# Attention with a LoRA gate on one core: row sums gathered by GpSimd and DMA, eleven probability buffers, gate weights loaded late, PSUM banks split 3 and 4

## The reference

```python
xn = layernorm(x)
q, k, v = xn @ wq, xn @ wk, xn @ wv          # 32 query heads, 8 key/value heads, 32 wide
k, v = repeat(k, 4), repeat(v, 4)            # four query heads share one key/value head
scores = where(causal, q @ k.T * 32**-0.5, min)
s = (softmax(scores) @ v) @ wo
lora = top-2 of 8 experts, rank 16, weights renormalised
g = silu(xn @ W_base.T + b_base + lora)
out = x + s * g
```

## Time and profile before

| | |
|---|---|
| median of three runs | 3545.49 us |
| profiled execution, its own time | 3544.42 us |
| its span, first to last instruction | 3542.6 us |
| project / attend / gate / output, roughly | 0 to 667 / 667 to 2774 / 2774 to 3180 / 3180 to 3543 us |
| TensorE matmuls busy | 3360.0 us, 95% |
| VectorE busy | 1873.0 us, 53% |
| ScalarE busy | 1435.3 us, 41% |
| GpSimd busy | 1291.0 us, 36% |
| mean granted TensorE clock | 0.975 |
| DMA on the queue of GpSimd | 117.45 MB, 14.3% of 16 engines |

### The profile page before, as it was taken

One profiled execution on the slowest core, in us unless ns is written; L12 is line 12 of the kernel. 1 busy time (PEld: TensorE's weight loads), 2 busy tenths in 40 slices (PEclk: granted clock), 3 DMA queues, 4 the chain that ended last, 5 costly groups with the idle time before them and its releaser, 6 DMA issues. The chain is left out here.

```text
span 3542.6 us, 63490 instructions
## 1 busy us (share of the span) xinstructions
PE 3360.0 (95%) x19200; PEld 2236.6 (63%) x19200; DVE 1873.0 (53%) x4613; ACT 1435.3 (41%) x2658; POOL 1291.0 (36%) x446
## 2 busy tenths in 40 slices
PE   6999999799999999999999999999999799989999
PEld 5888888555555555555555555555554588878887
DVE  5333332567667677667666676677763122223333
ACT  3222221155555556556555565566666110110000
POOL 0000000156666576565565575566667000000000
PEclk9999999699999999999999999999999899999999
DMA  6555544534534444444444444453533444445555
GB/s 224 158 160 179 170 155 133 147 82 106 126 97 112 114 102 108 109 102 116 101 108 115 96 117 110 98 126 98 120 88 93 135 160 144 141 132 178 190 192 175
DMA packets 278980, 461.98 MB, mean 130 GB/s; under 512 B 40352, under 2 KB 156064, under 8 KB 262816
## 3 DMA queue, kind: packets, MB, share of 16 engines
q1 hardware_dynamic: 258960, 328.32, 31.1%
q0 software_dynamic: 16128, 117.45, 14.3%
q10 hardware_dynamic: 3600, 12.58, 1.1%
HBM read 205.03 MB, written 134.74 MB: 96 GB/s over the span
## 5 line engine op out<-in xcount | busy, mean ns | idle before, releaser
L1030 ACT ACTIVATE probs<-cols_ps 128x512 f32<-128x512 f32 x2176 | 1148.8, 611 | 577.5 <-PE cols_ps L977 471.9
L1053 DVE TENSOR_REDUCE row_max<-rows_ps 128x1 f32<-128x512 f32 x1536 | 992.9, 681 | 374.3 <-PE rows_ps L894 372.8
L977 PE MATMUL cols_ps<-q_st,k_st 97*128 97x512 f32 x2176 | 909.3, 427 | 52.3 <-ACT probs L1030 36.3
L894 PE MATMUL rows_ps<-k_st,q_st 96*128 96x512 f32 (+3 forms) x2560 | 900.1, 381 | 28.6 <-DMA q_st<-scratch_q_hi 17.2
L859 POOL TENSOR_TENSOR added<-added,probs 128x2048 f32<-128x2048 f32 x192 | 898.8, 4681 | 26.9 <-ACT probs L1030 21.1
L977 PEld LDWEIGHTS cols_ps<-q_st,k_st 97*128 97x128 f32 x2176 | 412.6, 190 | 399.1 <-issue 221.6
L1057 DVE CUSTOM_DVE_ANT_0 masked_rows<-rows_ps,tri 128x128 bf16<-128x128 f32 (+3 forms) x1024 | 485.9, 484 | 237.2 <-PE rows_ps L894 233.8
L894 PEld LDWEIGHTS rows_ps<-k_st,q_st 96*128 96x128 f32 x2560 | 496.0, 194 | 167.2 <-DVE row_max L1053 69.7
L932 PE MATMUL o_ps<-probs,v_st 128*32 128x512 f32 (+3 forms) x5120 | 539.6, 540 | 2.6 <-ACT probs L1030 2.6
L859 POOL TENSOR_TENSOR added<-probs 128x2048 f32<-128x2048 f32 x48 | 220.0, 4583 | 629.8 <-PE cols_ps L977 614.6
L932 PEld LDWEIGHTS o_ps<-probs,v_st 128*32 128x32 f32 x5120 | 134.9, 110 | 269.1 <-issue 202.4
(11 more groups left out here) (105 smaller groups left out, 3150.4 us busy)
## 6 DMA issues: line engine op xcount, KB each, us to landing
dma_added<-probs POOLq DMA_DIRECT2D x112, 1024.0 KB, 6.9
q_st<-scratch_q_hi SPq DMA_DIRECT2D x128, 256.0 KB, 5.3
x_sb<-in_x SPq DMA_DIRECT2D x32, 512.0 KB, 4.0
scratch_xt_hi<-xt_hi SPq DMA_DIRECT2D x32, 512.0 KB, 6.0
scratch_xt_lo<-xt_lo SPq DMA_DIRECT2D x32, 512.0 KB, 6.8
scratch_q_hi<-out_hi SPq DMA_DIRECT2D x64, 256.0 KB, 2.5
scratch_q_lo<-out_lo SPq DMA_DIRECT2D x64, 256.0 KB, 2.9
q_st<-scratch_q_lo SPq DMA_DIRECT2D x64, 256.0 KB, 4.7
```

What stands on the lines that cost most here:

```text
L894: nc.tensor.matmul(rows_ps[rows_slot(k)][:, 0:keys], q_st[c][0:K1, h, i * P:(i + 1) * P], k_st[kbuf][0:K1, CH * p:CH * p + keys], start=Tr ...
L977: ins = nc.tensor.matmul(into, k_st[n.u][:, j * P:(j + 1) * P], q_st[c][:, :, i * P:(i + 1) * P], start=True, stop=not diagonal)
L1030: nc.scalar.activation(probs_of(c, j)[:, :, i * P:(i + 1) * P], cols_ps[cols_slot(AT_T[t])][:, :].rearrange("p (h q) -> p h q", h=NREP), A ...
L1053: nc.vector.tensor_reduce(into, bank[:, :], AX.X, ALU.max).then_inc(rows_free, 1)
```

## The change

1. **Banks and buffers**: `rows_ps` has three banks instead of four, `cols_ps` four instead of three, `probs` eleven buffers instead of six, in a plain ring.
2. **Sums**: every buffer is now in `ADDS` or `DMA_ADDS`; `REST` is gone. The exponentials of the first j of each list are written straight into the sum (`added[c % 2]`, `dma_added[c % 2]`, two of each), the others are added to it. GpSimd makes 3, 4, 7 and 9 additions for chunks 0 to 3 instead of 0, 3, 5 and 7; DMA makes 0, 2, 3 and 5 additions instead of 0, 0, 3 and 4 (of which one was a copy). The first addition waits for the W that reads the sum's buffer.
3. **Y** multiplies only one or two sums and stands behind the first visit of the next chunk, and the chain L1 to L4 moves with it. ScalarE's copy of the output (O) now comes ahead of Y and waits itself for the earlier store.
4. **Loop**: three chunks are peeled instead of two (`PEEL = 3`).
5. **Gate weights**: raw blocks are loaded by SP during the last group over the queries and keys that are no longer needed. ScalarE and VectorE split them at the start of `gate`, and the first tile of `gate` runs both halves beside each other, k by k. ScalarE's first loads of wo wait for the second tile's input.

```diff
-NROWS, NCOLS, NPROBS = 4, 3, 6
+NROWS, NCOLS, NPROBS = 3, 4, 11
...
-ADDS = [[], [0, 1, 2, 3], [0, 1, 3, 5, 6, 8], [0, 1, 3, 4, 6, 7, 9, 11]]
-DMA_ADDS = [[], [], [2, 4, 7], [2, 5, 8, 10]]
-REST = [[j for j in range(TPC * (c + 1)) if j not in ADDS[c] + DMA_ADDS[c]] for c in range(CPB)]
+ADDS = [[0, 1, 2, 3], [0, 3, 5, 6, 7], [0, 3, 5, 6, 8, 9, 10, 11], [0, 3, 5, 6, 8, 10, 12, 13, 14, 15]]
+DMA_ADDS = [[], [1, 2, 4], [1, 2, 4, 7], [1, 2, 4, 7, 9, 11]]
+RING = [(c, j) for c in range(CPB) for j in range(TPC * (c + 1)) if j not in ADDS[c][:1] + DMA_ADDS[c][:1]]
...
+def weighed_at(c, j):
+
+    return tiles_through(c, j - j % PER_VISIT + PER_VISIT - 1) + VISIT_AFTER - 1
+
+
 for _c in range(CPB):
-    for _j in range(0, TPC * (_c + 1), 2):
-        _t = tiles_through(_c, _j + 1) + VISIT_AFTER - 1
-        event(_t, "W", _c, _j)
+    for _j in range(0, TPC * (_c + 1), PER_VISIT):
+        event(weighed_at(_c, _j), "W", _c, _j)
+    event(weighed_at(_c, _j) + 2, "O", _c)
+
+    for _list, _kind in ((ADDS, "A"), (DMA_ADDS, "D")):
+        for _j in _list[_c][1:]:
+            event(max(tiles_through(_c, _j) - 1, weighed_at(_c, _list[_c][0])), _kind, _c, _j)
+for _c in range(CPB):
+
+    _t = weighed_at((_c + 1) % CPB, 0) + (0 if _c + 1 < CPB else NTG)
     event(_t, "Y", _c)
-    event(_t + 2, "O", _c)
...
-        PEEL = 2
+        PEEL = 3
...
         def probs_of(c, j):
-            return probs[probs_slot(J_OFF[c] + j)]
+            if j in ADDS[c][:1]:
+                return added[c % 2]
+            if j in DMA_ADDS[c][:1]:
+                return dma_added[c % 2]
+            return probs[probs_slot(RING.index((c, j)))]
...
+                total = added[c % 2]
                 pool.wait_ge(probs_ready, made_count(n, c, back, j))
-                if first:
-
-                    if sum_before(n, c) is not None:
-                        pool.wait_ge(cols_full, sum_before(n, c))
-                    other = probs_of(c, ADDS[c][0])
+                if j == ADDS[c][1]:
+                    pool.wait_ge(values_done, weighed_count(n, c, back, ADDS[c][0]))
...
-                parts = [(probs_of(cc, j), max(0, j - TPC * cc) * P) for j in REST[cc]]
-                if ADDS[cc]:
-                    pe.wait_ge(pool_added, n.lin(NADD, adds_through(cc, NJG) - back * NADD))
-                    parts = [(added, 0)] + parts
+                pe.wait_ge(pool_added, n.lin(NADD, adds_through(cc, NJG) - back * NADD))
+                parts = [added[cc % 2]]
                 if DMA_ADDS[cc]:
                     pe.wait_ge(dma_done, n.lin(16 * NDMA, 16 * (dma_adds_through(cc, NJG) - back * NDMA)))
-                    parts = parts[:1] + [(dma_added, 0)] + parts[1:]
+                    parts.append(dma_added[cc % 2])
...
@@ def gate @@
-            act.wait_ge(t_loaded[0], 64)
+            for k in range(NW):
+                nc.scalar.activation(w_hi[:, k, :], w_raw[:, k, :], ACT.Copy).then_inc(w_hi_ready, 1)
+            act.wait_ge(t_loaded[1], 64)
             load_ow(0)
...
+            for k in range(NW):
+                dve.wait_ge(w_hi_ready, k + 1)
+                nc.vector.tensor_sub(w_lo[:, k, :], w_raw[:, k, :], w_hi[:, k, :].bitcast(FP32)) \
+                    .then_inc(w_lo_ready, 1)
...
+            pe.wait_ge(t_loaded[0], 64)
+            pe.wait_ge(z_ready, 2)
+            for k in range(NW):
+                pe.wait_ge(w_lo_ready, k + 1)
+                for half in range(2):
+                    ins = step(0, half, k)
```

More of the change, by code:

```diff
@@ L618 @@
 NADD = sum(len(a) - 1 for a in ADDS if a)
-NDMA = sum(map(len, DMA_ADDS))
+NDMA = sum(len(a) - 1 for a in DMA_ADDS if a)
 def adds_through(c, j):
@@ L643, in attend @@
         NL = NREP * CH // P
-        q_st = [sb(f"q_st{i}", [K1 + 1, NREP, CH], FP32R) for i in range(CPB)]
-        k_st = [sb(f"k_st{i}", [K1 + 1, S], FP32R) for i in range(2)]
+        with nc.sbuf_tensor("gw_raw", [P, KT + 1, D], FP32) as gw_raw:
+            pass
+        q_st = [sb(f"q_st{i}", [K1 + 1, NREP, CH], FP32R) for i in range(CPB - 1)]
+        k_st = [sb("k_st0", [K1 + 1, S], FP32R)]
+        sb("gw_raw_end", [P, D])
+        q_st.append(sb("q_st_last", [K1 + 1, NREP, CH], FP32R))
+        k_st.append(sb("k_st1", [K1 + 1, S], FP32R))
         v_st = [sb(f"v_st{i}", [P, S // P, HD]) for i in range(2)]
@@ L648, in attend @@
         probs = [sb(f"probs{i}", [P, NREP, CH]) for i in range(NPROBS)]
-        added = sb("added", [P, NREP, CH])
-        dma_added = sb("dma_added", [P, NREP, CH])
+        added = [sb(f"added{i}", [P, NREP, CH]) for i in range(2)]
+        dma_added = [sb(f"dma_added{i}", [P, NREP, CH]) for i in range(2)]
         row_max = [sb(f"row_max{i}", [P, NREP, TPC, CPB]) for i in range(2)]
@@ L683, in attend @@
         l_inv_ready = sem("a_l_inv_ready")
-        l_inv_stored = sem("a_l_inv_stored")
+        l_inv_stored = [sem(f"a_l_inv_stored{i}") for i in range(2)]
         l_spread = [sem(f"a_l_spread{i}") for i in range(2)]
@@ L687, in attend @@
         o_stored = [sem(f"a_o_stored{i}") for i in range(2)]
-        gw_loaded = [sem(f"a_gw_loaded{i}") for i in range(2)]
-        gw_hi_ready = sem("a_gw_hi_ready")
-        gw_lo_ready = sem("a_gw_lo_ready")
+        gw_loaded = sem("a_gw_loaded")
         NW = KT + 1
@@ L741, in cols_free_count, with weighed_count @@
             return None if first_group(n) and before < 0 else cols_count(n, before)
[L743 to L747, removed]
+        def weighed_count(n, c, back, j):
+            return n.lin(NVG, visit_of(c, j) + 1 - back * NVG)
         def rows_count(n, ahead, k):
@@ L806, in run @@
                             load_q(n.lin(1, 0 if c == 0 else 1), (c - 1) % CPB)
-                    elif kind == "K" and not last_group:
+                        else:
+                            load_gw(2 * c - 2)
+                            load_gw(2 * c - 1)
+                    elif kind == "K":
                         if not isinstance(n.pair, int) or n.pair > 0 or n.u > 0:
                             wait_apart(sp, values_done, n.lin(NVG, 0), passed)
-                        load_kv(n.lin(1, 1), 1 - n.u)
+                        if last_group:
+                            for k in range(2 * CPB - 2, NW):
+                                load_gw(k)
+                        else:
+                            load_kv(n.lin(1, 1), 1 - n.u)
                     elif kind == "M":
@@ L927, in weigh @@
                         pe.wait_ge(v_loaded[vbuf], n.pair * 16 + 16)
-                pe.wait_ge(probs_ready, made_count(n, cc, back, j0 + 1))
-                for j in (j0, j0 + 1):
+                pe.wait_ge(probs_ready, made_count(n, cc, back, j0 + PER_VISIT - 1))
+                for j in range(j0, j0 + PER_VISIT):
                     q0 = max(0, j - TPC * cc) * P
@@ L1101, in _, with gate @@
             over_stages(dve, run)
-def gate(nc, b_base, sc, w_hi, w_lo, wo, ow_hi, ow_lo):
+        return gw_raw
+def gate(nc, b_base, sc, w_raw, wo, ow_hi, ow_lo):
     ctx = ExitStack()
```

134 lines of the change are left out of this document (63 added, 71 removed).

## The result

The changed kernel takes 3590.49 us, the median of four runs (3586.37 to 3593.47), against 3545.61 us for the kernel before on the same chip: ratio 1.0125, 95% interval 1.0104 to 1.0147. It is slower by 45 us, clear of the noise, where 3476 us was forecast.

A forecast was written before the change was run, and what follows sets the result against it. TensorE was taken to set the pace, busy 1992 of the attention's 2098 us. From 3544.4 us, gains of 178 and losses of 110 gave 3476 us; range 3400 to 3545 us.

The forecast's parts named there:

- The row sums: TensorE's Y in the attention: seven sums a group, 6.0 us instead of 12.5, saving 104 us over 16 groups.
- the wait of ScalarE for the DMA's buffer: In the attention, eleven buffers end ScalarE's waits for buffers the DMA still reads: 30 us gained.
- the gate: Gate's first tile: splitting weights runs beside TensorE's wait for input, so only 1 us is lost.
- The third row bank: Row scores, three banks instead of four: VectorE has 0.60 us less behind a visit, 88 us lost, bounds 0 and 192.
- 88 + 6 - 10: Bank swap: 88 us lost on row scores, 6 on the 84 rows before the first T, 10 gained for T.
- the fourth bank for T: Transposed scores: one T and the S behind it issue earlier, 10 us gained, bounds nothing and 54.9.
- the one on GpSimd and Y: GpSimd's additions fit, with 2.6 us spare before Y of chunk 3; 5 us lost for 64 Y.
- the third rival: GpSimd comes late for Y behind slow DMA additions, deciding from a landing of about 10 us: 3604 us, chance 0.09.
- the end of the attention: Last chunk 3: most of the final 11.8 us of additions stand behind the last T, about 10 us lost.
- The check that GpSimd's work fits: GpSimd's additions and DMA issues in a group take 93 of some 124 us, so they fit.
- 12 us won: Y after ScalarE's stalls: two sums at the lower clock, 1.7 us, avoided in seven groups; bounds 0 and 27 us.
- The second rival: Bank swap eats the gain: every visit loses 0.60 us, 192 instead of 88, 3580 us; chance 0.07.

The follow-up runs named there:

- the other lists: Changed kernel with DMA additions three blocks apart and chunk 3's j = 13 to 15 in Y: 3573 us with three row banks and four transposed, 3478 with four and three.
- rest_all: `banks43_rest3` with the last DMA addition of chunks 1 to 3 given to GpSimd, and last buffers of chunks 1 and 2 multiplied in Y: 3415.55 us, ratio 0.9618.
- the additions are apart: Kernels with the changed kernel's DMA additions set three blocks apart by new lists; `banks43_spaced` is the first of them, 3531.84 us.
- before_banks34: Kernel before with only the change's bank split, three row banks and four transposed: 3593.94 us, ratio 1.0138.
- banks43_spaced: Changed kernel with four row banks, three transposed, DMA additions three blocks apart, one of chunk 3's moved to GpSimd: 3531.84 us, ratio 0.9971.
- banks43_rest3: `banks43_spaced` with j = 13 to 15 of chunk 3 multiplied by TensorE in Y instead of added by GpSimd: 3478.01 us, ratio 0.9802.
- rest3_banks34: `banks43_rest3` with three row banks and four transposed instead of four and three: 3572.77 us, ratio 1.0067 to the kernel before.

## Why the prediction was wrong

**The row sums** were right: 101 us measured, 104 forecast. So was the wait of ScalarE for the DMA's buffer, which is gone, and the gate, at 1.3 us for 1.

**The third row bank** was right as a mechanism. The gap of VectorE behind a full visit grew by the 0.60 us that was forecast (0.86 to 1.46), the visit by 0.70. The price depends on what else is late. The forecast's terms for the swap are 88 + 6 - 10 = 84 us net; measured, also net, it is 50 us in the kernel before, 22 in the changed kernel and 95 with the other lists. The 10 us of the fourth bank for T were not measured by themselves.

**The step that failed is the one on GpSimd and Y**, put at 5 us between "nothing" and the third rival, with the end of the attention at 10. Without the swap, the change was to bring 152 us, and it brought some 4 us with three and four banks, within the noise, and lost 28 with four and three. `rest_all`, the version in which Y no longer waits for either helper, is 132 us under the kernel before, although its Y keeps TensorE busy for 152.0 us instead of 118.5. Four things in the step were wrong.

- The landing of a DMA addition was taken from the earlier trace rows as 6.9 us, but that median mixes copies and additions. The additions alone took 7.3 us, as long as the distance of 7.3 us between two issues, so the rival's "against it" was a misreading, and the 31.9 us that GpSimd already stood behind them were not looked at. In the changed kernel the landing is 7.9 us in the median and up to 14.7.
- The check that GpSimd's work fits (93 of 124 us in a group) was made on the mean, while the additions lie close together at the end of a chunk and the issues stand in the same queue.
- Y was looked at as waiting for GpSimd alone, not for the last DMA addition, for which only chunk 2 was worked out. In the kernels where GpSimd was relieved it is the DMA for which Y waits, 39 to 104 us, until `rest_all` takes the last additions out.
- The rival's own sum does not come out. At a landing of 10 us one wait of 2.7 us already uses up the 2.6 us to spare, not two or three; and at 12 us three waits of 4.7 less 2.6 make 11.5 us, not 8. It was said to decide from a landing of about 10 us. It costs with a median of 7.9, since a few slow landings are enough to hold up a queue with 2.6 us to spare.

**The waits that were put at nothing or overlooked** can be listed against the forecast, on TensorE's own rows: Y waits 45.1 us for GpSimd and 10.9 for the DMA (not in the list above) where 15 were foreseen for queue and end, some 41 too few; the turn of the loop 24.1 - 13.4 = 11 us; the row of shifts for chunk 3, 11.7 us. The last two do not stand by themselves: where the additions are apart the waits for the row of shifts are gone from the list and the turn is back at 14 to 16 us. A fourth part is the clock. Its mean over the span fell from 0.975 to 0.968 where the prediction had it rise. With the levels of 1.2 and 2.4 GHz, half of the time at the lower one is lost: a mean of 0.975 means 2 x 0.025 x 3543 = 177 us there and 0.968 means 230, an estimate of some 26 us more lost, and not 12 us won. The clock was low behind long stands of TensorE, as at the end above. Together 41 + 11 + 12 + 26 + 12 = 102 us of the 114 between 3476 and 3590. This list is read off the trace and not tested item by item. It counts the row bank at the 88 us of the forecast, while undoing the swap in this kernel brings only 22, so that the sum comes close to 114 is in part luck.

**The second rival** named the right bank and the wrong sum: it takes the bank alone to 192 us, and no run showed that. In the changed kernel neither of the two causes can be blamed alone: with the bank given back it is still 28 us slower than the kernel before, with the sums eased it is 26 us slower, and with both it is 68 us faster.

The page "TensorEngine Tiling (Array Packing)" of the Trainium skill, which the second rival drew on, says under PSUM Bottleneck that tiling speeds up TensorE but not the emptying of PSUM. The runs do not bear it out as the reason here. Thinning out Y with four row banks left the row scores waiting 88.1 + 8.8 us for VectorE, against 69.7 + 8.9 before; taking the bank with the old Y (`before_banks34`) made it 238.7 + 74.6. It is the number of banks that did it.

## What to carry to other kernels

Work taken off the engine that sets the pace is only won if what now makes its input is on time: work out for each wait when the last of its inputs lands, on the queue it is issued from, not whether the helper's total fits. Take durations from rows of the one operation that you need, not from a median over two kinds. In this kernel a DMA issue that waited for the one before it held up all of GpSimd's additions behind it, so leave more than the slowest landing seen between two of them, and keep the last pieces of a sum on the engine that needs them. And when undoing a suspect changes little, undo two at a time before it is let off: here each alone brought some 20 us and both 112.

## What the runs showed of the hardware that was not expected

A DMA addition into a buffer in SBUF took markedly longer than a plain copy of the same 1 MB: 6.8/7.3/9.6 us (least, median, most) against 4.5/4.6/5.3, both in the kernel before. In no run did an addition land in under 6.8 us. The slowest took 9.6 us with 80 additions in the kernel, 9.1 with 96 (`rest_all`), 12.2 with 144 (`banks43_spaced`) and 14.7 with 160 (the changed kernel); the load around them differs too. Additions over three quarters of the columns, 768 KB, took 10.6 us in the median where whole ones of 1 MB took 7.4 in the same kernel (`banks43_spaced`, 16 and 128 of them); in `banks43_rest3` it was 8.6 against 7.5, in `rest3_banks34` 10.1 against 7.5. The turn of TensorE's loop took 2.2 us on the mean in the kernel before and 5.5 us with the same instructions and the turn one chunk later, but 2.2 to 2.7 us at that later place in the kernels with the additions apart; why was not found.
